# Routing spread over the last projections down and over attention's steps, with norm factors shared and ScalarE applying them

## The reference

```
x = x + retention_blocks(layernorm(x))   # 2 layers (retention, then 128 -> 512 -> 128), and a last
                                         # layer_norm with gain lnf_g and shift lnf_b
x = x + moe(layernorm(x))                # 8 experts, each token goes to its 2 largest gate logits
x = x + attention(layernorm(x))          # 16 heads of 8 channels, causal, softmax
x = x + moe(layernorm(x))                # the same experts again

moe: logits = x @ gate_w; w, i = top_k(softmax(logits), 2); w /= w.sum()
     out = sum over experts of w * ((silu(x @ w1) * (x @ w3)) @ w2)
```

## Time and profile before

| | us |
|---|---|
| median of 3 runs (1049.19 to 1051.26) | 1049.51 |
| the profiled execution's own time | 1046.18 |
| its span | 1044.3 |
| PE busy | 702.2 |
| DVE busy | 602.1 |
| ACT busy | 331.3 |
| POOL busy | 329.7 |

### The profile page before, as it was taken

One profiled execution on the slowest core, in us unless ns is written; L12 is line 12 of the kernel. 1 busy time (PEld: TensorE's weight loads), 2 busy tenths in 40 slices (PEclk: granted clock), 3 DMA queues, 4 the chain that ended last, 5 costly groups with the idle time before them and its releaser, 6 DMA issues. The chain is left out here.

```text
span 1044.3 us, 19748 instructions
## 1 busy us (share of the span) xinstructions
PE 702.2 (67%) x6652; PEld 477.3 (46%) x6652; DVE 602.1 (58%) x1825; ACT 331.3 (32%) x565; POOL 329.7 (32%) x654
## 2 busy tenths in 40 slices
PE   1789887889883119997215398378569863089991
PEld 0355455555562018996111144234234432078991
DVE  7978545889288706664504376246347527146763
ACT  2232324333421014442320156145245541034440
POOL 0123300134331756776430001101100115746771
PEclk9899998999975559999555599779779985589996
DMA  9101595111200115553321101101100000145554
GB/s 225 43 26 57 118 190 123 42 42 42 56 1 10 47 50 154 159 166 112 112 107 71 53 3 47 82 11 42 79 17 3 3 1 32 51 119 150 156 162 133
DMA packets 99569, 80.89 MB, mean 77 GB/s; under 512 B 7383, under 2 KB 91418, under 8 KB 98730
## 3 DMA queue, kind: packets, MB, share of 16 engines
q1 hardware_dynamic: 94926, 70.25, 24.9%
q0 software_dynamic: 4544, 9.38, 2.7%
HBM read 54.44 MB, written 23.40 MB: 75 GB/s over the span
## 5 line engine op out<-in xcount | busy, mean ns | idle before, releaser
L1153 DVE TENSOR_REDUCE rmax<-PA 128x1 f32<-128x512 f32 (+3 forms) x256 | 120.9, 490 | 151.1 <-PE PA L1791 143.3
L728 POOL DMA_INDIRECT outs_dram<-va,ids x78 | 93.8, 1202 | 54.8 <-POOL ids L724 27.8
L1086 DVE SCALAR_TENSOR_TENSOR pm<-PB,invb,decay 128x512 f32<-128x512 f32 x78 | 58.1, 744 | 61.9 <-ACT decay L1400 61.9
L1751 PE MATMUL PC<-ffn_w,pm 128*128 128x128 f32 x624 | 88.0, 284 | 6.9 <-DMA ffn_w<-in_w 4.8
L1789 PE MATMUL PA<-mqb,idb 128*128 128x128 bf16 x256 | 60.6, 238 | 45.1 <-DMA qst<-qst 29.9
L1791 PE MATMUL PA<-kst,qst 96*128 96x512 bf16 (+3 forms) x256 | 84.5, 336 | 0.0
L1751 PEld LDWEIGHTS PC<-ffn_w,pm 128*128 128x128 f32 x624 | 75.7, 191 | 11.1 <-DMA ffn_w<-in_w 7.2
L1392 ACT ACTIVATE kv_b<-P 128x256 f16<-128x256 f16 x78 | 29.9, 383 | 156.3 <-PE P L1730 152.2
L713 POOL DMA_INDIRECT rows_dram<-va,idx x64 | 64.4, 1006 | 45.7 <-DVE va L1039 26.8
L1467 ACT ACTIVATE pm<-PB 128x1024 f32<-128x1024 f32 (+1 forms) x64 | 44.9, 702 | 101.9 <-PE PB L1814 101.8
L1789 PEld LDWEIGHTS PA<-mqb,idb 128*128 128x128 bf16 x256 | 25.5, 100 | 107.6 <-issue 58.2
(11 more groups left out here) (214 smaller groups left out, 1585.4 us busy)
## 6 DMA issues: line engine op xcount, KB each, us to landing
ffn_w<-in_w SPq DMA_DIRECT2D x78, 256.0 KB
rows_dram<-wall SPq DMA_DIRECT2D x1, 8385.0 KB, 46.3
X<-in_w SPq DMA_DIRECT2D x32, 256.0 KB, 2.9
proj_w<-rows_dram SPq DMA_DIRECT2D x78, 65.0 KB
qst<-parts_dram SPq DMA_DIRECT2D x12, 384.0 KB
kst<-parts_dram SPq DMA_DIRECT2D x12, 384.0 KB
X<-in_x SPq DMA_DIRECT2D x8, 256.0 KB, 4.8
R<-outs_dram SPq DMA_DIRECT2D x4, 512.0 KB, 3.8
```

Source lines behind the costliest of these rows:

```text
L728: nc.gpsimd.indirect_dma_start(out=outs_dram, out_offset=bass.IndirectOffsetOnAxis(ap=ids[:, k % YB:k % YB + 1], axis=0), in_=ysb[:, k % Y ...
L1086: nc.vector.scalar_tensor_tensor(out=eT[:, k % 2, :, :].rearrange("p f n -> p (f n)"), in0=PB[:, k % 2, :], scalar=invb[:, k % 2:k % 2 + 1 ...
L1153: nc.vector.tensor_reduce(rmax[:, i, h % HG:h % HG + 1], PA[:, n % 2, 0:(i + 1) * P], AX_X, ALU.max).then_inc(pair_sb[n % 2], 1)
L1751: ins = mm(PC[:, k % 2, 0:D], eT[:, k % 2, f, :], w2b[k % WB2][:, f, :], start=f == 0, stop=f == FB - 1)
```

## The change

It moves work between engines and places, and computes the same.

- When the blocks are left, DVE makes the factors of R's section s and of X's section s-1 in one run of small steps (leave_factors), and ACT applies them (leave_normalize). POOL adds the shift to X ahead of time (add_shift), and so has two instructions left for a section.
- The first routing starts earlier: TensorE routes section 0 ahead of the last quarter of section 2's projection down, and routes section 1 and counts section 0 ahead of the last quarter of section 3's. DVE ranks section 0 behind leave_factors(1).
- The second routing of sections 0 to 2 lies in attention's steps of sections 1 to 3, with uses "mt" (transposes, step 14), "rt" (gate_w, step 16) and "ct" (counts, step 22), DVE's route at step 18 and choose_slots at step 25, and POOL's eight scatters behind norm_factors of the same section. Only section 3 is left after attention.

```diff
-    plan += routes(0) + att(0) + att(1) + routes(1)
+    plan += routes(0) + att(0) + att(1)
+    plan += [("turn", LNM2, SEQ - 1), ("router", 1, SEQ - 1), ("count", 1, SEQ - 1)]
...
-        out += {3: [("tr", s - 1, 1)], 5: [("ao", s - 1)], 7: [("wo", s - 1)]}.get(v, [])
+        out += {3: [("tr", s - 1, 1)], 5: [("ao", s - 1)], 7: [("wo", s - 1)], 14: [("mt", s - 1)],
+                16: [("rt", s - 1)], 22: [("ct", s - 1)]}.get(v, [])
...
+            def add_shift(s):
+                r = slice(TPS * s, TPS * s + TPS)
+                pool.wait_ge(x_back[s], 16)
+                nc.gpsimd.tensor_tensor(X[:, r, :], X[:, r, :], lnf[:, 1, :].unsqueeze(1).to_broadcast([P, TPS, D]),
+                                        ALU.add).then_inc(shift_sb, 1)
...
-                for s in range(SEQ):
+                for s in range(SEQ) if m == 0 else (SEQ - 1,):
                     scatter_rows(m, s)
...
                         if s + 2 < SEQ:
                             part_rests(s + 2)
                         norm_factors(A + SEQ + s)
+                        scatter_rows(1, s)
...
+            def leave_factors(i):
+                jobs = ([(R, i)] if i < SEQ else []) + ([(X, i - 1)] if i >= 1 else [])
+                if i >= 1:
+                    dve.wait_ge(left_sb, i)
...
+                w = TPS * len(jobs)
+                for j, (src, s) in enumerate(jobs):
+                    for k in range(TPS):
+                        ins = nc.vector.bn_stats(st6[:, TPS * j + k, :], src[:, TPS * s + k, :])
...
+                if m == 0:
+                    choose_slots(m, 0)
+                    route(m, 1)
+                    leave_factors(SEQ)
+                    for s in range(2, SEQ):
+                        choose_slots(m, s - 1)
+                        route(m, s)
+                else:
+                    route(m, SEQ - 1)
                 choose_slots(m, SEQ - 1)
...
+                        if v == 18 and s >= 1:
+                            route(1, s - 1)
+                        if v == 25 and s >= 1:
+                            choose_slots(1, s - 1)
...
+            def leave_normalize(i):
+                act.wait_ge(fac_sb, i + 1)
+                jobs = ([(R, i, lnf_sb)] if i < SEQ else []) + ([(X, i - 1, xn_ready)] if i >= 1 else [])
...
                         if v == HV - 4 and s >= 1:
                             normalize(LNM2, s - 1)
+                            high_rows(1, s - 1)
+                        if v == 20 and s >= 1:
+                            exp_logits(1, s - 1)
...
                     for k in range(TPS):
+                        if k == TPS - 1 and layer + 1 == LAYERS and s >= 2:
+                            route(0, s - 2)
+                            if s == SEQ - 1:
+                                count(0, 0).then_inc(ring_ps, 1)
```

More of the change, by code:

```diff
@@ L473, in wait_pair, with wait_router, wait_count @@
             eng.wait_ge(pair_sb[PAIR[key] % 2], PAIR[key] // 2 + 1)
+        def wait_router(eng, m, s):
+            if m == 1 and s + 1 < SEQ:
+                wait_pair(eng, "rt", s)
+            else:
+                wait_ring(eng, "router", m, s)
+        def wait_count(eng, m, s):
+            if m == 1 and s + 1 < SEQ:
+                wait_pair(eng, "ct", s)
+            else:
+                wait_ring(eng, "count", m, s)
         def wait_front(eng, what, c):
@@ L748, in _ @@
             for s in range(SEQ):
+                add_shift(s)
+            for s in range(SEQ):
                 leave_blocks(s)
@@ L1714, in feed_forward @@
                     down(s)
-                    if layer + 1 == LAYERS and s == SEQ - 2:
-                        route(0, 0)
                 pe.wait_ge(f1_sb, SEQ * FB * (layer + 1))
@@ L1756, in experts @@
                     pe.wait_ge(f2_up, LAYERS * SEQ)
-                for s in range(1, SEQ):
-                    route(m, s)
-                    count(m, s - 1)
-                count(m, SEQ - 1)
+                if m == 0:
+                    for s in range(2, SEQ):
+                        route(m, s)
+                        count(m, s - 1).then_inc(ring_ps, 1)
+                else:
+                    route(m, SEQ - 1)
+                count(m, SEQ - 1).then_inc(ring_ps, 1)
                 wait_ring(pe, "count", m, SEQ - 1)
@@ L1873, in run @@
                             turns(LNC, key[0], pair("turn", *key)).then_inc(pair_ps, 1)
+                        if what == "mt":
+                            turns(LNM2, key[0], pair("mt", *key)).then_inc(pair_ps, 1)
+                        if what == "rt":
+                            wait_pair(pe, "mt", *key)
+                            router(1, key[0], pair("rt", *key)).then_inc(pair_ps, 1)
+                        if what == "ct":
+                            count(1, key[0], pair("ct", *key)).then_inc(pair_ps, 1)
                         if what in "qk":
```

158 lines of the change are left out of this document (100 added, 58 removed).

## The result

| series | kernel before, median us | changed kernel, median us | ratio, 95% interval |
|---|---|---|---|
| first | 1050.38 | 1037.62 | 0.988 (0.983 to 0.993) |
| second (e1) | 1052.60 | 1060.96 | 1.008 (1.005 to 1.011) |
| third (g3) | 1050.99 | 1039.81 | 0.987 (0.983 to 0.991) |

The prediction was 1033.5 us, within 1025 to 1043, faster with 0.94. Two series bear that out, with less gained than forecast; one turns it round. One of the first series' four runs of the kernel before is a slow one (1125.42 us): its ratio leaves it out, and without it that median is 1049.51.

What follows compares the result with a forecast made beforehand. GpSimd's row scatters were taken to bound both routings and TensorE ordinary attention groups; -3.6 + 17.6 - 30.0 = -16.0 us made 1030.2 from the profiled 1046.18, or 1033.5 for the median; range 1025 to 1043.

Steps and rivals of the forecast that it cites:

- A: Leaving the blocks and first routing: the first scatter comes at 337.2 against 340.80, so -3.6 us.
- B: Attention's sections 1 to 3: added routing work, stops of TensorE and later rests cost +17.6 us, between 8 and 28.
- C: Second routing's tail: only section 3 remains behind attention, last scatter at 882.5 against 912.54, so -30.0 us.
- rival 5: Blocks' stage keeps the full clock: leaving the blocks and first routing gain 11 us, time 1026; chance 0.08.
- rival 2: Projections down wait longer or their clock costs more: that stage loses 5 us, time 1042; chance 0.13.
- so each stops it by about 1: Attention: route and choose_slots, about 3 us each on VectorE, each stop TensorE by about 1 us.
- Before step 25: Attention, section 1: 1.9 + 1.1 + 1 = 4.0 us are added ahead of choose_slots, delaying scatters and rests.
- Rival 4: Attention, steps 14 to 31: added waits drop TensorE's clock, making it slower than before, up to 1064; chance 0.04.
- signs of being wrong: Last scatters at other distances, attention growing under 8 or over 28 us, or TensorE's ordinary-group clock falling from 1.00.
- Rival 1: Attention: the rests' delay is absorbed in TensorE's idle time, attention costs 11.9 us, time 1028; chance 0.15.
- Rival 3: Attention: VectorE slows the scatters, to 1.58 us each in section 1, 5 us more, time 1038.5; chance 0.12.
- The rule of the Trainium skill: Attention: VectorE's two-port copies lock out GpSimd's descriptors, eight scatters costing section 1 another 20 us; not taken into the sum.

Runs made afterwards that it cites:

- e1: The changed kernel itself run again, in the second series: 1060.96 us, ratio 1.008 to the kernel before.
- g3: The changed kernel run a third time, on a third chip: 1039.81 us, ratio 0.987 to the kernel before.
- e2: Changed kernel with only the new leaving of the blocks and first routing, second routing wholly behind attention as before: 1051.65 us, ratio 0.999.
- g1: As f4, but sections 2 and 3 routed behind attention, and sections 1 to 3 scattered behind the last norm factors: 1030.56 us, ratio 0.979.
- f3: Kernel before plus ten VectorE instructions with unread results at step 18 of sections 1 and 2: 1055.19 us, ratio 1.005.
- e3: Changed kernel with GpSimd's eight scatters of section 0 behind the rests of section 3 in place of ahead: 1057.29 us, ratio 1.005.
- e4: As e3, with VectorE's route and choose_slots cut into single instructions or pairs, one ahead of every use: 1049.12 us, ratio 0.998.
- f2: Changed kernel with all 32 scatters of the second routing behind attention, ranking left in attention's steps: 1064.89 us, ratio 1.013.
- f4: Changed kernel with section 0 routed and scattered in section 2's wait for the stacks, sections 1 and 2 in section 3: 1046.31 us, ratio 0.995.
- g2: As g1, but section 1 is routed behind attention too: 1035.36 us, ratio 0.985.
- series e and f: The follow-up runs named with e, all on one chip, and those named with f, on a second chip.

## Why the prediction was right, and where it was wrong

The three terms, from the two profiles of the first series:

| term | predicted | measured |
|---|---|---|
| A, leaving the blocks, first routing | -3.6 | -3.7 |
| B, attention | +17.6 | +27.3 |
| C, the tail | -30.0 | -30.1 |
| sum | -16.0 | -6.5 (profiled executions: -6.4) |

By the profiles the miss is 9.6 us (1039.77 against 1030.2), all of it in B. That the median, 1037.62, comes within 4.1 us of 1033.5 is in part luck: the medians differ by 5.5 us more than the two profiled executions do.

- **C was right in each step.** "GpSimd is the bound" held; from the end of normalize to the end of the last scatter 20.6 us, worked out as 21.
- **A was right in the first series**: first scatter 337.12 for 337.2, projection down 326.64 for 326.9. The lower clock that it took for both projections was granted (0.50 from 303.6 to 327), so rival 5 falls, and rival 2's longer waits did not come. It is not a property of the kernel, though: in e2 and in g1 it is near 0 (first scatter 340.2 and 340.8).
- **B's wrong step is "so each stops it by about 1".** I booked 1 us, a third of a piece, although the row that I gave for it has a wait of 2.09 us behind five small steps. route stopped TensorE for 2.95 and 2.96 us, choose_slots for 1.91 in section 2. In section 2 I had 5.0 us and it was 11.7: 2.4 in the group with transposes and logits, 5.7 in route's and 3.6 in that of choose_slots. In section 1 the step "Before step 25" with its 4.0 us fails in the same way, and makes 12.6 of 9.7; the path that I gave it, through the scatters to the rests, bound only for its last 1.6 us, since the rests' own input came at 730.26. Section 3, without maxima, was 2.9 us as worked out.
- **Why a third was wrong.** VectorE was busy 9.37 of 11.80 us in such a group. It had 2.4 us to give, and only between maxima, each of which a bank waits for. I counted TensorE's 95% as the bound and VectorE's 79% as room. f3 shows it alone: a piece of 2.1 us made the group 2.1 longer at the full clock. e3's row, 3.4 us more at the full clock, is the longer piece paid in full, and e4's shows that cutting it up does not change it.
- **The clock.** Rival 4 had the right mechanism and too little of it: not slower than before by it, but 2.3 us in route's group of section 2, where the granted clock fell to 0.80 behind the stop. With that, one of the prediction's own signs of being wrong came true, a clock under 1.00 in an ordinary group. The argument against the rival, "the clock is 1.00 in the group of steps ahead", looked at a group without a stop of 3 us. Nor does such a stop settle it: in e3 the clock stayed at 1.00 behind one of the same length.
- **Rival 1, the delay is absorbed:** it was not, the wait moved whole, by 9.7 us. But the scatters ahead of the rests were the cause of at most 1.6 of them; in e3, without them, the rests wait as long for their own inputs.
- **Rival 3, scatters slowed by VectorE's work, falls:** 0.96 to 1.08 us each in attention. The rule of the Trainium skill that I weighed (SBUF — State Buffer, "SBUF: two separate sides") was not seen at work there; outside attention single scatters took up to 1.61 us (f3), and none the 3.1 that was weighed. What happened in the second series is the other way round: TensorE, ScalarE and VectorE stood still while scatters ran.
- **What no case of mine had** is that. The first profile of the kernel before gives no sign of it. In the second series the changed kernel was slower than before, where I gave 0.04, and by another mechanism than rival 4's.

What is shown: the waits appear in attention only with scatters (f2 without and f4 with, on one chip; e2 without and e1 with, on another), while they run or within 2 us behind the last; VectorE's pieces are paid in full; the clock takes 2.3 us more in route's group. What stays open: how a scatter holds up other engines (no run separates a signal that comes late from instructions that come late), why some chips or loadings show it and others don't, and when the clock falls behind a stop.

## What to carry to other kernels

Work that is spread into the shadow of another stage is paid for by whichever engine goes in step with that stage's bound: add it to the busy time of every engine in the group, and take the whole of it where the sum nears the group's length. Look first for stretches in which everything waits for a DMA: eight scatters and their whole ranking cost nothing there (f4, g2), while in the sections with maxima the same cost some 12 us each, and 2.9 in the one without. And repeat a result on another chip before a gain of 1% is believed.

## What the runs showed of the hardware

- Waits of 3 to 7.7 us on TensorE, ScalarE and VectorE, with their inputs ready and no releaser in the trace, while GpSimd's indirect scatters ran. The series e and f showed them in attention, the first series and g3 did not; the length of a scatter (0.96 us and 0.30 of gap) is the same in both.
- Behind a stop of 3 us in an otherwise full stretch TensorE's granted clock can fall for part of the group, and need not: 17.50 us at 0.80 (after) and 15.16 at 1.00 (e3) for the same work with the same stop.
- "issue" in brackets can hide an ordinary wait: TensorE's 4.88 us before 879.23 end 0.15 us after VectorE has written what it reads.
- The same program, loaded again in a second series, was 2.2% slower in all of its seven runs (1056.7 to 1064.5 against 1033.8 to 1040.6), while the kernel before moved by 0.2%.
